# Eight expert tiles listed early and interleaved with the attention tail

## The chip, the cores and the metric
One core of a Trainium2 chip runs the whole program in one launch. The metric is the device time of the launch in microseconds (us); the time before is the median of three runs.

## What is computed
Two layers over x of shape (32, 128, 256), that is 4096 tokens of width 256. Each layer adds a gated cross attention (16 heads of 16) and then a gated mixture of experts (8 experts, two per token) to x:

```python
x = x + tanh(g_xattn) * attention(layernorm(x), ctx)
h = layernorm(x)
x = x + tanh(g_ffn) * experts(h)     # top 2 of 8, by a router on h
```
In layer 0 an expert is a relu network of width 1024 with biases and the gates are a softmax of the two best logits. In layer 1 the attention is causal and masked, an expert is silu(gate) * up of width 512, and the gates come from masked softmaxes (two exponentials over all eight logits).

## The kernel before
There are five instruction lists, written by hand, one for each engine (TensorE, VectorE, ScalarE, GpSimd, SyncE); each engine runs its own in order and waits on semaphores. Each layer has two stages.

**Attention** runs over steps s from FIRST = -8 to LAST = 148 (`pe_attention`, L492, and its like for the other engines). A unit is four heads of one batch, 128 units in all; a step handles unit s, and the pieces of the neighbouring units that are due. `grp(s, k)` and `bat(s, k)` say whether the piece of a group (4 batches, 8 groups) or of a batch is due k steps behind its start. The last units end at step 127; behind it come sums, the last outputs, and the routing of the last groups.

**Routing** of a group (`Part`, L114) starts at step `e0`: the reciprocal root of the variance (started on VectorE, 12 small instructions on GpSimd, L903 to L909, for groups 0 to 6), the normed rows XR (L1208), two transposes, the logits (L566), maximum and index (L970, L975), SEL (L988), gates (L993 to L1032), ranks by two matmuls (L572), the running counts CR and the row numbers PI (L1039 to L1060). GpSimd then scatters the rows to the expert's region in DRAM, one DMA_INDIRECT per 128 rows (L1403), eight for a group. The last group is routed in two halves, and its root is made on VectorE. `dve_lists` (L1233) makes, when all groups are counted, where the rows of each tile start: tiles 0 to 7 are the first tile of each expert, tiles 8 to 38 come from the list, whose expert and start SyncE reads into registers (L1437, L1455). `pad` (L785) writes 256 rows behind the end of each expert's rows.

**Experts** runs over NT = 39 tiles of 256 rows. The work of tile i on TensorE (L627): the transposes of tile i + 1's rows (`pe_turn_x`, L578), the up projection of tile i in four pieces q, the down projection of tile i - 1. Every product is three matmuls, high x high, high x low, low x high (L420 to L422). ScalarE rounds the weights to their high parts (`act_w`, L791), and makes relu or silu and the hidden high parts (L812, L826). VectorE makes the low parts of the rows, of the hidden values and of weight quarters 1 and 2; GpSimd makes the low parts of quarters 0 and 3 (`low_w`, L1273) and scatters the outputs (`pool_y`, L1406). Tile i + 1's up projection needs quarter 0's low part; the down projection needs quarters 2 and 3. SyncE's iteration i (L1552) asks for the rows of tile i + 2 first and then for biases and the weight quarters, each once its buffer is free. Two row buffers and two weight generations are in turn.

Ahead of the experts stage TensorE waits until all banks are free (`banks_out`, L396) and runs WARM2 = 48 matmuls on nothing (L630). SyncE asks for tile 0's rows when the last group's scatters have landed; the pads of experts 1 to 3 are issued by ScalarE, the others by SyncE.

Of the kernel before, what the change touches and what calls it, by code (L numbers as in the profile page):

```python
# [15 lines left out]
T = B * S  # L16
E = 8
# [5 lines left out]
NT = (2 * T - E) // TS + E  # L23
ROW = D + 2
# [10 lines left out]
WARM, WARM1, WARM2 = 8, 28, 48  # L35
# [8 lines left out]
C_TOK = C_TILE + NT - E  # L44
# [4 lines left out]
def constants():  # L49
# [9 lines left out]
    c[:, C_TILE:C_TILE + NT - E] = np.arange(NT - E)  # L59
# [51 lines left out]
class Part:  # L111


    def __init__(self, g, lo, hi):  # L114
# [3 lines left out]
        late = g >= NG - 2  # L118
# [3 lines left out]
            self.e1 + k for k in ((1, 1, 1, 1, 1, 2, 2, 3, 3, 3) if late else (1, 2, 2, 3, 3, 4, 3, 4, 5, 6)))  # L122
# [19 lines left out]
def bat(s, k):  # L142
    b, m = divmod(s - k, 4)
    return b if m == 0 and 0 <= b < B else None


def program(nc, A):
    ctx = ExitStack()
    with ctx:  # L149
# [37 lines left out]
        su = sb("su", [128, NT - E])  # L187
# [25 lines left out]
        tge = sb("tge", [128, NT - E, E])  # L213
        tv = sb("tv", [128, 4, NT - E])
        tvi = sb("tvi", [128, 2, NT - E], I32)
# [7 lines left out]
        HS = [v.rearrange("p (z f n) -> p z f n", z=2, f=8) for v in (PTR[:, 0:4096], WR[:, :, :, :, :].rearrange("p w z t n -> p (w z t n)"))]  # L223
# [3 lines left out]
        b2s = XRf[:, 6 * D:8 * D].rearrange("p (r d) -> p r d", r=2)  # L227
# [3 lines left out]
        XN = U2[:, 1024:2048].rearrange("p (g d) -> p g d", g=G)  # L231
        XR2 = U2[:, 2048:2048 + 2 * G * ROW].rearrange("p (k g d) -> p k g d", k=2, g=G)
# [11 lines left out]
        SB_, PTB, OB, BK, BO_, HBK, YB, XB = PS[0:3], PS[3:5], PS[5], PS[6], PS[7], PS[0:4], PS[4:6], PS[6:8]  # L244
# [4 lines left out]
        def xr(g):  # L249
            return XR if g < NG - 1 else XR2  # L250

# [48 lines left out]
        p_rs2 = mark("p_rs2", [k for k in prts if k[1] < NG - 1])  # L300
# [8 lines left out]
        v_pd, v_tl = mark("v_pd", LL), mark("v_tl", LL)  # L309
# [27 lines left out]
        def uses_bk(L):  # L337
            out = []
            for s in range(FIRST, LAST):
# [18 lines left out]
            return out  # L358
# [36 lines left out]

        def banks_out(w, L):  # L396

            w.wait_ge(*a_p[L, NU - 1])
            w.wait_ge(*a_pt[L, NU - 1])
            w.wait_ge(*v_on[L, B - 1])  # L400
            w.wait_ge(*a_v[L, NG - 1, 1])
            w.wait_ge(*v_rk[(L,) + PARTS[-1].key])
            w.wait_ge(*v_lg[(L,) + PARTS[-1].key])
            if L == 0:
                w.wait_ge(*v_xup[0, B - 1])
# [85 lines left out]

        def pe_attention(e, w, L):  # L492
            pe_first(e, w, L)
            for s in range(FIRST, LAST):
                if 0 <= s < NU:
                    i, bank = s, pt_place["p", s]
                    w.wait_ge(*a_p[L, i])
                    turn_free(w, L, "p", i)
                    for h in range(4):
                        ins = e.transpose(bank[:, h * 128:(h + 1) * 128], PB[:, i % 3, h], ident)  # L500
                    ins.then_inc(*m_t(L, i))
                if 0 <= s + 4 < NU:
                    i = s + 4
                    b, m, z = i // 4, (i // 2) % 2, i % 2
                    g, j, bank = b // G, b % G, SB_[i % 3]
                    w.wait_ge(*v_q[L, g, 1])
                    if i < 2:
                        w.wait_ge(*a_v[L, 0, i])
                    w.wait_ge(*d_k[key_queue(L, b)][L, b, 7])
                    if i >= 3:  # L510
                        w.wait_ge(*a_p[L, i - 3])
# [8 lines left out]
                if (b := bat(s, 6)) is not None:  # L520
# [3 lines left out]
                    for n in range(4):  # L524
                        ins = e.transpose(bank[:, n * 128:(n + 1) * 128], OS[:, n * 128:(n + 1) * 128], ident)
# [1143 lines left out]
```

## Time and profile before
| | |
|---|---|
| median of three runs | 1687.52 us (1686.19 to 1691.3) |
| profiled execution, first to last instruction | 1689.9 us |
| TensorE busy | 1575.0 us, 93% |
| VectorE, ScalarE, GpSimd busy | 71%, 73%, 49% |
| mean granted TensorE clock | 0.966 |
| DMA | 256.56 MB, mean 152 GB/s |

Times are us from the span's start. A granted clock of 1 is 2.4 GHz, 0.5 is 1.2 GHz. The chip's profile page gives only this span for the profiled execution; the three runs are separate ones. Layer 0's attention fills 0 to about 356, its experts 410 to about 880, layer 1's attention then runs to about 1256 and its experts from 1318 to the end.

### The profile page before, as it was taken

Reading aid. Unit: us, or ns where it says so; the run is one execution under the profiler, and the core shown is the slowest. Engines: PE = TensorE matmul, PEld = TensorE weight load, DVE = VectorE, ACT = ScalarE, POOL = GpSimd, SP = SyncE. Lnnn points to the kernel's source line nnn. Section 1 sums busy time; section 2 is a strip of 40 time slices with the busy share of each in tenths; the row PEclk is TensorE's granted clock in tenths of the full one; section 3 lists DMA queues with packets and bytes.
Section 4 is the critical chain, followed back from the end, with each engine's and each line's share of the span. In section 5 each row is a group of like instructions: output and inputs, shape, how many; then the busy total and the mean of one; then the engine's idle time right before and its main releaser. Section 6 shows DMA issues by size and latency. Waiting matters only on the chain. (4 is left out here: it accounts for less than half of the span.)

```text
span 1689.9 us, 37219 instructions
## 1 busy us (share of the span) xinstructions
PE 1575.0 (93%) x12832; PEld 1424.2 (84%) x12832; DVE 1194.5 (71%) x2829; ACT 1232.1 (73%) x2859; POOL 826.4 (49%) x887
## 2 busy tenths in 40 slices
PE   7999999976999999999988999999984999999996
PEld 5788888865999999999986777777773899999996
DVE  5677777755777777777766788888857566766664
ACT  5888888853888888888863877777771577777774
POOL 3224444343556565656552113333323477777776
PEclk9999999987999999999998999999995999999999
DMA  3222222135877777778742223333232788788883
GB/s 110 54 50 75 75 76 76 51 95 148 261 235 235 224 230 228 232 226 236 225 141 78 72 82 104 107 104 104 62 90 77 200 225 242 222 230 231 226 233 99
DMA packets 208988, 256.56 MB, mean 152 GB/s; under 512 B 29555, under 2 KB 156788, under 8 KB 208800
## 3 DMA queue, kind: packets, MB, share of 16 engines
q1 hardware_dynamic: 185408, 217.95, 44.2%
q0 software_dynamic: 21120, 34.39, 7.9%
q10 hardware_dynamic: 2272, 1.85, 0.4%
q8 instruction: 102, 1.67, 0.4%
q14 instruction: 86, 0.70, 0.1%
HBM read 194.54 MB, written 45.74 MB: 142 GB/s over the span
## 5 line engine op out<-in xcount | busy, mean ns | idle before, releaser
L1276 POOL TENSOR_TENSOR KXR<-U,KXR 128x1024 fp32r<-128x1024 f32 (+1 forms) x156 | 355.2, 2277 | 276.9 <-ACT KXR L795 276.9
L420 PE MATMUL ps<-QR,KXR 128*128 128x256 f32 x1248 | 360.4, 289 | 0.8 <-DVE QR L1280 0.7
L422 PE MATMUL ps<-QR,KXR 128*128 128x256 f32 x1248 | 354.2, 284 | 0.0
L421 PE MATMUL ps<-QR,KXR 128*128 128x256 f32 x1248 | 354.0, 284 | 0.0
L795 ACT ACTIVATE KXR<-U 128x1024 fp32r<-128x1024 f32 (+1 forms) x312 | 287.4, 947 | 73.2 <-PE ps L422 49.4
L743 ACT ACTIVATE U<-ps,mx 128x128 f32<-128x128 f32 x1024 | 299.0, 405 | 20.3 <-DVE mx L1153 20.3
L420 PEld LDWEIGHTS ps<-QR,KXR 128*128 128x128 f32 x1248 | 240.6, 193 | 1.4 <-DVE QR L1280 1.3
L421 PEld LDWEIGHTS ps<-QR,KXR 128*128 128x128 f32 x1248 | 240.4, 193 | 0.0
L422 PEld LDWEIGHTS ps<-QR,KXR 128*128 128x128 f32 x1248 | 240.0, 192 | 0.0
L1153 DVE TENSOR_REDUCE mx<-ps 128x4 f32<-128x512 f32 x256 | 174.3, 684 | 69.3 <-PE ps L422 37.1
L1276 DVE TENSOR_TENSOR KXR<-U,KXR 128x1024 fp32r<-128x1024 f32 (+1 forms) x156 | 175.0, 1160 | 25.6 <-ACT KXR L795 25.5
L1403 POOL DMA_INDIRECT xs_scr<-XR,PI x112 | 109.8, 980 | 133.6 <-DVE PI L1060 104.6
L500 PE MATMUL ps<-cst,U 128*128 128x128 f32 x1024 | 163.5, 283 | 10.0 <-DVE U L1163 9.5
L750 ACT ACTIVATE U<-ps 128x512 f32<-128x512 f32 x256 | 166.5, 650 | 7.4 <-PE ps L500 7.4
L500 PEld LDWEIGHTS ps<-cst,U 128*128 128x128 f32 x1024 | 117.3, 143 | 48.1 <-issue 23.6
L821 ACT ACTIVATE U<-ps,b1s 128x256 f32<-128x256 f32 x312 | 130.4, 473 | 29.9 <-PE ps L422 29.9
L1307 DVE TENSOR_TENSOR PTR<-U,PTR 128x512 fp32r<-128x512 f32 x80 | 101.0, 1298 | 60.6 <-ACT PTR L832 60.6
L420 PE MATMUL ps<-KXR,PTR 128*128 128x256 f32 x480 | 136.1, 284 | 3.6 <-ACT U L810 1.5
L1307 DVE TENSOR_TENSOR WR<-U,WR 128x512 fp32r<-128x512 f32 x76 | 97.9, 1326 | 56.6 <-ACT WR L832 56.6
L421 PE MATMUL ps<-KXR,PTR 128*128 128x256 f32 x480 | 135.8, 283 | 0.0
L422 PE MATMUL ps<-KXR,PTR 128*128 128x256 f32 x480 | 135.8, 283 | 0.0
L1419 POOL DMA_INDIRECT out<-U,xi x78 | 121.1, 1552 | 20.0 <-issue 19.7
(206 smaller groups left out, 4043.3 us busy)
## 6 DMA issues: line engine op xcount, KB each, us to landing
U<-in_wpack SPq DMA_DIRECT2D x234, 512.0 KB, 4.4
U<-in_wpack SPq DMA_DIRECT2D x78, 256.0 KB, 4.2
KXR<-U SPq DMA_DIRECT2D x504, 32.0 KB
U<-xs_scr SPq DMA_DIRECT2D x39, 258.0 KB, 4.5
U<-xs_scr SPq DMA_DIRECT2D x39, 257.0 KB, 4.7
U<-in_ctx_t SPq DMA_DIRECT2D x16, 512.0 KB, 5.7
U<-ys_scr SPq DMA_DIRECT2D x32, 256.0 KB, 3.4
XR<-in_L_ffn_b SPq DMA_DIRECT2D x39, 128.0 KB, 3.9
```

Source lines behind the costliest of these rows:

```text
L420: e.matmul(o, wh, xh, start=first, stop=False)
L421: e.matmul(o, wh, xl, start=False, stop=False)
L422: return e.matmul(o, wl, xh, start=False, stop=done)
L500: ins = e.transpose(bank[:, h * 128:(h + 1) * 128], PB[:, i % 3, h], ident)
L743: ins = e.activation(PB[:, i % 3, h], SB_[i % 3][:, h * 128:(h + 1) * 128], ACT.Exp, bias=mx[:, i % 4, h:h + 1], scale=-1.0)
L750: e.activation(PT[:, i % 3].rearrange("p h k -> p (h k)"), pt_place["p", i][:, :], ACT.Copy).then_inc(*a_pt(L, i))
L795: e.activation(w_cols(L, WH, n), w_raw(L, n), ACT.Copy).then_inc(*a_w[n](L, i))
L821: ins = e.activation(HB[:, r, f], HBK[q][:, z * 256:z * 256 + 256], ACT.Relu, bias=b1s[:, r, f:f + 1])
L1153: e.tensor_reduce(mx[:, i % 4], SB_[i % 3][:, :].rearrange("p (h k) -> p h k", h=4), AX.X, ALU.min).then_inc(*v_mx(L, i))
L1276: e.tensor_tensor(w_cols(L, WL, n), w_raw(L, n), hi, ALU.subtract).then_inc(*l_w[n](L, i))
L1307: ins = e.tensor_tensor(low[:, 2 * q:2 * q + 2], HB[:, i % 2, 2 * q:2 * q + 2], high[:, 2 * q:2 * q + 2], ALU.subtract)
L1419: ins = e.indirect_dma_start(ys_d[1], at, yo[:, r, a, :], None, bounds_check=T - 1, oob_is_err=False, compute_op=ALU.add)
```

## The change
- KE = 8 tiles are listed from the counts of the first GE = 5 groups (20 batches), in steps 101 to 104 (`dve_lists_early`). Only full tiles are taken, so none needs padding; an assertion says that eight always exist. The rest, tiles 8 to 38, is listed from the final counts less those tiles, in steps 147 to 149. NT stays 39.
- Attention's own loop ends at START = 128. Steps 128 to 149 are run inside the expert loop, four to a tile, so inside tiles 0 to 5: step 128 + 4 i + k is piece k of tile i (`late`). On each engine they stand between the pieces of a tile.
- The rows of tiles 0 and 1 are requested in step 117, transposed in steps 124 and 126; two weight quarters of tile 0 are rounded there too, and their low parts made (steps 125 and 126, on GpSimd and VectorE).
- The bank wait and the 48 matmuls go; the tile transposes take turns in the two banks that attention's projections and the routing use.
- The last group is routed whole, its reciprocal root on GpSimd like the others.
- All eight pads are issued by SyncE in iteration 6 of the experts stage, and the rows of tile 8 are requested at its end. The expert and start of every tile come from registers.
- The output biases and part of the hidden buffers move to other memory.

```diff
+GE, KE = 5, 8
-PARTS = [Part(g, 0, G) for g in range(NG - 1)] + [Part(NG - 1, 0, G // 2), Part(NG - 1, G // 2, G)]
+PARTS = [Part(g, 0, G) for g in range(NG)]
-FIRST, LAST = -8, 148
+FIRST, START, LAST = -8, 128, 150
+LIST0, TX, LIST1 = 101, (124, 126), 147
...
+def late(i, k):
+
+    s = START + 4 * i + k
+    return s if s < LAST else None
...
         def pe_experts(e, w, L):
-            banks_out(w, L)
-            for n in range(WARM2):
-                e.matmul(SB_[2][:, :], QR[:, 0, 0, 0, 0:128], QR[:, 1, 0, 0, :], start=True, stop=True)
-            for i in range(2):
-                pe_turn_x(e, w, L, i)
-            for i in range(NT):
-                if i and i + 1 < NT:
+            for q in range(4):
+                pe_up(e, w, L, 0, q)
+                pe_late(e, w, L, 0, q)
+            for i in range(1, NT):
+                if i + 1 < NT:
                     pe_turn_x(e, w, L, i + 1)
-                pe_up(e, w, L, i)
-                if i:
-                    pe_down(e, w, L, i - 1)
+                for q in range(4):
+                    pe_up(e, w, L, i, q)
+                    if q % 2:
+                        pe_late(e, w, L, i, q // 2)
+                for half in range(2):
+                    pe_down(e, w, L, i - 1, half)
+                    pe_late(e, w, L, i, 2 + half)
             pe_down_last(e, w, L)
...
+            for s in range(FIRST, START):
+                act_step(e, w, L, s)
+                for i in range(2):
+                    if s == TX[i]:
+                        act_w(e, w, L, 0, i)
+                        act_turn_x(e, w, L, i)
...
+            for s in range(FIRST, START):
+                dve_step(e, w, L, s)
+                for i in range(2):
+                    if s == TX[i] + 1:
+                        dve_turn_x(e, w, L, i)
+                if s == TX[1]:
+                    low_w(e, w, L, 0, 1)
...
         def dve_experts(e, w, L):
-            dve_lists(e, w, L)
-            low_w(e, w, L, 0, 1)
...
+                    if i == 0:
+                        dve_late(e, w, L, 0, q)
+                    elif q == 1:
+                        dve_late(e, w, L, i, 0)
                 if L == 1:
                     dve_hidden(e, w, 1, i, 3)
+                if i:
+                    dve_late(e, w, L, i, 1)
                 if i + 1 < NT:
                     low_w(e, w, L, i + 1, 1)
+                if i:
+                    dve_late(e, w, L, i, 2)
                 low_w(e, w, L, i, 2)
+                if i:
+                    dve_late(e, w, L, i, 3)
...
         def pool_experts(e, w, L):
-            low_w(e, w, L, 0, 0)
             for i in range(NT):
                 if i:
                     low_w(e, w, L, i - 1, 3)
+                pool_late(e, w, L, i, 0)
                 if i >= 2:
                     pool_y(e, w, L, i - 2)
+                pool_late(e, w, L, i, 1)
                 if i + 1 < NT:
                     low_w(e, w, L, i + 1, 0)
+                for k in (2, 3):
+                    pool_late(e, w, L, i, k)
...
         def sp_experts(e, w, L):
-            pad(e, w, L, 0)
...
-            for x in range(4, E):
-                pad(e, w, L, x)
             for i in range(NT):
+                if L == 1 and i == 1:
+                    sp_store_x(e, w, NG - 1)
+                if i == KE - 2:
+                    for x in range(E):
+                        pad(e, w, L, x)
-                if L == 0 and i == 2:
+                if L == 0 and i == KE + 2:
                     sp_ahead(e)
...
-                if i + 2 < NT:
+                if i + 2 < NT and i + 2 != KE:
                     sp_fetch_x(e, w, L, i + 2)
...
                 if i + 1 < NT:
                     sp_fetch(e, w, L, i + 1, 2, sp_expert(e, w, L, i + 1))
+                if i + 2 == KE:
+                    sp_fetch_x(e, w, L, KE)
```
ScalarE's list has the late steps at the same places as VectorE's (`act_late`). GpSimd's step code and the step code of the other engines is the old code moved into functions (`pe_step`, `act_step`, `dve_step`, `pool_step`).

## Rows read from the trace of the kernel before

**Rows 1.** 40 us stretches: busy us (x instructions) per engine, PEclk, DMA share, GB/s
```profile
core 0: us, PE busy (x) PEld busy (x) DVE busy (x) ACT busy (x) POOL busy (x), PEclk, DMA share, GB/s
360.00:400.00 40.00, 24.37 (x140) 19.86 (x139) 25.10 (x141) 7.61 (x18) 16.61 (x21) 0.62 0.17 58
...
600.00:640.00 40.00, 40.00 (x337) 40.00 (x337) 30.24 (x35) 31.63 (x55) 22.43 (x13) 1.00 0.77 224
...
1280.00:1320.00 40.00, 24.21 (x102) 19.79 (x103) 23.43 (x125) 7.57 (x15) 17.37 (x18) 0.66 0.39 128
...
1440.00:1480.00 40.00, 40.00 (x337) 40.00 (x337) 27.21 (x57) 30.07 (x65) 30.59 (x19) 1.00 0.83 236
```

**Rows 2.** TensorE's timeline, layer 0: start, us, engine, line, operation, [idle before <-releaser]
```profile
359.18 0.66 PE L558 MATMUL ps<-cst,XR 128*128 128x128 f32 x4 [2.97 <-DVE XR L1208]
...
394.54 13.22 PE L630 MATMUL ps<-QR 128*128 128x512 f32 x48 [0.28 <-DVE RK L965]
...
494.05 0.60 PE L585 MATMUL ps<-cst,U 128*128 128x128 f32 x4
...
506.00 0.60 PE L585 MATMUL ps<-cst,U 128*128 128x128 f32 x4
```

**Rows 3.** TensorE's timeline, layer 1
```profile
1267.48 0.64 PE L488 MATMUL ps<-U,VA 128*32 128x128 f32 x16
...
1383.50 0.60 PE L585 MATMUL ps<-cst,U 128*128 128x128 f32 x4
...
1392.57 0.60 PE L585 MATMUL ps<-cst,U 128*128 128x128 f32 x4
```

**Rows 4.** ScalarE's timeline, layer 0's tail
```profile
362.60 1.05 ACT L775 ACTIVATE XR<-XR 128x1024 f32<-128x1024 f32 x1
```

**Rows 5.** VectorE's timeline: routing in both tails, hidden pieces of two tiles
```profile
370.90 0.23 DVE L965 COPY RK<-ps 128x64 f32<-128x64 f32 x1
...
373.01 0.17 DVE L1060 CAST PI<-PF 128x8 int32<-128x8 f32 x1
...
584.01 4.44 DVE L1307 TENSOR_TENSOR PTR<-U,PTR 128x512 fp32r<-128x512 f32 x3 [1.08 <-ACT PTR L832]
...
1267.59 0.19 DVE L959 COPY LG<-ps 128x32 f32<-128x32 f32 x1 [3.48 <-PE ps L566]
...
1269.44 0.19 DVE L988 TENSOR_TENSOR SEL<-MM 128x32 f32<-128x32 f32 x1
...
1271.61 0.18 DVE L1009 TENSOR_SCALAR rt<-rt 128x32 f32<-128x32 f32 x1
...
1480.18 0.42 DVE L1309 TENSOR_TENSOR WR<-ps,WR 128x256 fp32r<-128x256 f32 x1 [1.42 <-ACT WR L834]
```

**Rows 6.** GpSimd's timeline: reciprocal root, scatters, output scatters, low weights
```profile
351.08 0.22 POOL L903 TENSOR_TENSOR rs<-rsi 128x4 f32<-128x4 f32 x1
...
354.19 0.20 POOL L909 TENSOR_TENSOR rs<-rs 128x4 f32<-128x4 f32 x1
...
374.84 0.97 POOL L1403 DMA_INDIRECT xs_scr<-XR,PI  x1 [0.30 <-issue]
...
581.67 1.26 POOL L1417 DMA_INDIRECT ys_scr<-U,xi  x1 [0.15 <-issue]
...
584.23 2.45 POOL L1276 TENSOR_TENSOR KXR<-U,KXR 128x1024 fp32r<-128x1024 f32 x1
...
1477.40 1.56 POOL L1419 DMA_INDIRECT out<-U,xi  x1 [0.16 <-issue]
...
1480.27 2.98 POOL L1276 TENSOR_TENSOR KXR<-U,KXR 128x1024 fp32r<-128x1024 f32 x1
```

**Rows 7.** SyncE's timeline: four pads in a row, the rows of a tile
```profile
409.10 4.76 SPq L788 DMA_DIRECT2D xs_scr<-cst  x4
...
580.12 0.38 SPq L1468 DMA_DIRECT2D U<-xs_scr  x1
```

**Rows 8.** DMA issues of the page: tile rows in layer 0, KB each, us to landing
```profile
U<-xs_scr SPq DMA_DIRECT2D x39, 257.0 KB, 4.7
```

**Rows 9.** ScalarE's timeline, start of layer 1's experts
```profile
1318.85 1.28 ACT L824 ACT_TABLE_LOAD   x1
```

More of the change, by code:

```diff
@@ L117, in __init__ @@
         self.e0 = 16 * g + 4 * hi + 9
-        late = g >= NG - 2
+        fast = g >= NG - 2
         self.lt = (self.e0 + 4, self.e0 + 5)
@@ L338, in uses_bk, with uses_step @@
             out = []
-            for s in range(FIRST, LAST):
+            for s in range(FIRST, START):
+                uses_step(L, s, out)
+                for i in range(2):
+                    if s == TX[i]:
+                        out.append((("tx", i), v_x[L, i]))
+            for k in range(4):
+                uses_step(L, late(0, k), out)
+            for i in range(1, NT):
+                if i + 1 < NT:
+                    out.append((("tx", i + 1), v_x[L, i + 1]))
+                for k in range(4):
+                    if (s := late(i, k)) is not None:
+                        uses_step(L, s, out)
+            return out
+        def uses_step(L, s, out):
                 for name, at, empty in (("xt", X0, v_xt), ("q", Q0, v_q), ("k", K0, v_k), ("v", V0, a_v)):
@@ new lines, in pe_up, with pe_rows, pe_down @@
+            ins.then_inc(*m_h(L, i, q))
+        def pe_rows(e, w, L, i, f, a):
+            nf, c = NFs[L], (2 * F0, 4 * F1)[L] + f * D
+            w.wait_ge(*v_h[L, i, f if L else f // 2])
+            w.wait_ge(*l_w[2 + 2 * f // nf][L, i])
+            high, low = (hs(i, z, f, f + 1)[:, 0, a * 128:a * 128 + 128] for z in range(2))
+            return three(e, YB[a][:, 0:D], (high, low), (WH[:, c:c + D], WL[:, c:c + D]), f == 0, f == nf - 1)
+        def pe_down(e, w, L, i, half):
+            nf = NFs[L]
@@ L1315, in dve_gated, with dve_late @@
             e.tensor_tensor(up, HB[:, i % 2, q], up, ALU.mult).then_inc(*v_hm(i, q))
+        def dve_late(e, w, L, i, k):
+            if (s := late(i, k)) is not None:
+                dve_step(e, w, L, s)
         def dve_experts(e, w, L):
-            dve_lists(e, w, L)
-            low_w(e, w, L, 0, 1)
-            for i in range(2):
-                dve_turn_x(e, w, L, i)
             for i in range(NT):
@@ L1406, in pool_y, with pool_attention, pool_late @@
+        def pool_attention(e, w, L):
+            pool_first(e, w, L)
+            for s in range(FIRST, START):
+                pool_step(e, w, L, s)
+                if s == TX[0] + 1:
+                    low_w(e, w, L, 0, 0)
+        def pool_late(e, w, L, i, k):
+            if (s := late(i, k)) is not None:
+                pool_step(e, w, L, s)
         def pool_y(e, w, L, i):
```

848 lines of the change are left out of this document (456 added, 392 removed).

## The prediction
> **What bounds the kernel now.** I read the stretches of 40 us first. In the expert stages TensorE is busy for the whole stretch (40.00 of 40, 337 matmuls, so 0.119 us each); at 360 to 400 and at 1280 to 1320 it is busy for 24 us of 40 and its granted clock is 0.62 and 0.66 [rows 1]. These two stretches are the tails between attention and experts. Then I read TensorE's own timeline there. Layer 0: its attention work thins out at 356; its next matmul, at 359.18, follows 2.97 us of idleness; at 394.54 come 48 matmuls that only keep the clock up (13.2 us); tiles 7 and 8 start at 494.05 and 506.00 [rows 2]. Layer 1: the sum of the last unit is at 1267.48, tiles 7 and 8 start at 1383.50 and 1392.57 [rows 3]. A tile takes 11.95 us in layer 0 (100 matmuls) and 9.07 in layer 1 (76). The eight tiles ahead of tile 8 are the stretch that the change rearranges; behind it nothing changes. So I compute when tile 8 starts in each layer and compare.
>
> **The gross gain.** What is left of the tail (steps 128 to 149) is a few us of TensorE work: 4.1 us in layer 0 and 3.3 in layer 1 behind tile 0 (transposes, logits, ranks, the last output projection), and in tile 0 some 3 and 1.5. In layer 1 the first up projection could start at about 1268.0, where the last sum was. In layer 0 it is later than that sum. ScalarE ends the copy at 363.65 [rows 4]; behind it stands the new rounding of weights (1.05 us, the same 128x1024 form of copy); VectorE now waits for it inside attention to form the low part (1.2), then does its step 127 (1.3), on whose X update the bank of the second tile transpose waits (0.6); then the last transposes and the logits (2.3). That gives 370.0. Without any further wait tile 8 would start at 370.0 + 8.9 + 7 x 11.95 + 4.1 = 466.7 in layer 0, 39.3 us earlier than now, and at 1268.0 + 7.3 + 7 x 9.07 + 3.3 = 1342.1 in layer 1, 50.5 us earlier. Sum 89.8 us. The 48 matmuls per layer and the half groups' second square root are in this sum and are not counted again.
>
> **What it gives back.** Each engine runs its list in order, and the late steps stand between the pieces of a tile.
>
> *Tiles 0 and 1.* The ranks of group 6 are made in step 129. VectorE: 2.0 us from the logits' copy to SEL, 2.3 us from the rank copy to the row numbers, in layer 1 another 2.2 us for the gates [rows 5]. ScalarE waits in its step 128 for those gates and holds back the hidden columns. I come to the row numbers 15.1 us behind tile 0's start in layer 0 and 16.0 in layer 1. Then GpSimd issues four scatters (0.97 + 0.30 each, so 5.1 us), forms the low weights of tile 0's last quarter (2.4; half of it in layer 1), issues four more and forms tile 2's first quarter (2.45 to 2.98) [rows 6]. Tile 2 starts at +30.1 and +30.2, against 21.2 and 16.8 without waits: 8.9 and 13.4 lost.
>
> *Tile 2.* Step 137 has VectorE start group 7's reciprocal root and GpSimd do 12 instructions, 3.3 us [rows 6]. VectorE gets there when its four hidden pieces and the statistics are done, 11.9 us into the tile in layer 0 (the pieces q1 to q3 end at 588.4, and that tile starts at 506.00 + 6 x 11.95 = 577.7, so 10.7 us into it) [rows 2, 5] and 9.4 in layer 1. The low weights of tile 3's first quarter are queued on GpSimd behind it: 11.9 + 3.3 + 2.45 = 17.7, wanted at 12.3, and 15.3 against 9.4. Lost 5.4 and 5.9.
>
> *Tiles 4 and 5.* Step 144 is the routing of group 7. It stands behind the second hidden piece, so TensorE, done with its up projection at 6.2, waits for SEL until about 9.4 (8.2 in layer 1, where the first piece is ready at 1480.6, in a tile that starts at 1392.57 + 9 x 9.07 = 1474.2, so 6.4 us into it) [rows 3, 5]. The row numbers come at +17.8 and +18.8, since the hidden pieces, the gates and one low part stand between. Behind them on GpSimd: four scatters 5.1, low weights 2.4 (1.3), two scatters 2.5, two output scatters 2.55 (3.4), two scatters 2.5, low weights 2.45 (2.7) [rows 6]; 17.5 us in each. Tile 6 can start at +35.3 and +36.3, against 24.8 and 19.0: 10.5 and 17.3 lost. GpSimd is busy for 30.59 of 40 us in layer 1 already [rows 1].
>
> *Tile 8's rows.* Now the rows of a tile are requested at the start of the iteration two tiles ahead, 580.1 in the tile of 577.7, so 2.4 us into it and 9.5 before TensorE turns them [rows 7]. For tile 8 the change requests them at the end of iteration 6, behind all eight pads, and TensorE turns them at the start of iteration 7. On SyncE: start 3.0, eight pads at 1.19 (four took 4.76) 9.5, bias loads 2.3, four weight loads and the rows 5.7: issued at +20.5 in layer 0, landing 4.7 us later [rows 7, 8], at +25.2, where TensorE is ready at +11.6. In layer 1 there are no bias loads: I take +22.5 against +8.7. Lost 13.6 and 13.8. This is the surest term, since every price in it is a row.
>
> *Clock.* After an idle gap the granted clock is half: the tails show 0.62 and 0.66 [rows 1]. Where TensorE is not the one waited for, a slow matmul costs nothing; behind the long wait at tile 8 I take 1.5 us per layer. Bounds: 0, and 27 for the rival below.
>
> *Small terms.* In layer 1 the gates' Exp now stands between Silus: two changes of table and back, 1.28 us each [rows 9], within ScalarE's waits above, nothing more. The Trainium skill (ScalarE: Activation LUTs, What ACT_TABLE_LOAD costs) adds a drain and says about 2.66 us per switch; by it the sum would be some 3 us longer at two switches on the chain, and no row here shows the drain. The early lists (22 small VectorE instructions in steps 101 to 104, about 0.2 us each in chain, so 4.4 us a layer) lie beside attention, where TensorE leads in layer 0 and VectorE is close in layer 1; I take 2 us in all, bounds 0 and 9. SyncE reads the expert from a register in tiles 0 to 7, which it did not; it has the time, 1.15 us an issue, except in the term above. The burst of layer 1's loads, moved from tile 2 to tile 10, costs its 1.0 us outside the stretch. Scatters and pads, 4 MB a layer, join a DMA load of 0.77 [rows 1]; I take nothing, bounds 0 and 6, as the pads' own issue is already the slowest part.
>
> A low-weight instruction on GpSimd takes 2.45 us in layer 0 and 2.98 in layer 1, where VectorE's work overlaps it otherwise [rows 6]. The Trainium skill (SBUF — State Buffer, Who interferes with whom) says that a VectorE instruction with two SBUF inputs and a GpSimd one exclude each other for a whole instruction; by it VectorE's routing, with two small inputs in most instructions, could hold GpSimd back at each of its pieces, 0.5 us by the difference of the two rows, 4 to 6 us over both layers. I have it in the range only.
>
> **The sum.** Given back, layer 0: 8.9 + 5.4 + 10.5 + 13.6 + 1.5 = 39.9; layer 1: 13.4 + 5.9 + 17.3 + 13.8 + 1.5 = 51.9. With 2.0 and 1.0 it is 94.8 against 89.8, so 5.0 us slower. The profiled execution spans 1689.9 us; 1694.9. The median of the runs, 1687.5, lies 2.4 below that execution: 1692.5. A measurement of this kernel tells about 0.3%, 5 us, from no change, so this is within it, at the slow edge.
>
> **Rivals.**
> *Faster.* The routing waits (50.1 us over tiles 0 to 6 without the root) overlap more than I chain them, for instance because ScalarE and VectorE are ahead when a late step comes. For it: all three have idle time in layer 0 (VectorE 9.8, ScalarE 8.4, GpSimd 17.6 of 40 us, rows 1). Against: the lists are in order, and the waits come from order, not from load. The clock, the root and tile 8's rows stay. If half of the 50.1 go: 1667; if all: 1642. Chance 0.36.
> *Slower, by the clock.* TensorE is stopped at four places per layer, and each stop puts it at half clock as in the two tails. Tiles 0 to 7 hold 96 and 73 us of its work; if a third of it runs at 1.2 GHz, 56 us more, of which I take half to fall into waits: +27, 1719. It decides when the granted clock of these tiles is below 0.85. For it: 0.62 in a stretch with 24 us of work [rows 1]. Against: the stops are short beside a tile's 11.9 us of matmuls. The Trainium skill (TensorE: Matmul & The Clock Gate, HAM oscillation) tells of this pattern, where repeated gaps put the array back to the low clock each time. Chance 0.24.
> *Forecast.* The waits eat the gain, 1680 to 1706. Chance 0.40, the likeliest single case.
> That fewer tiles are listed is excluded: eight full tiles always exist in five groups, and the number of tiles stays 39.
>
> **How the numbers follow.** Forecast 1692. The range takes in half of the routing waits and most of the all-go case below (1645), and the clock rival with its DMA bound above (1722). Over 5 us faster: 0.38, the first rival and the low edge of my case; within: 0.20, from my case; slower: 0.42, the rest of it and the second rival.
>
> **What would show it.** Right: no idle stretch as in the two tails, but TensorE waits at the starts of tiles 2 and 3 and 6 for GpSimd's low weights, and some 13 us in each layer for DMA of the tile's rows at one transpose; DMA_INDIRECT of the routing back to back on GpSimd in front of these; the first up projection near 370 and 1268. Wrong: that 13 us wait absent, or the waits on GpSimd together under 25 us, or a granted clock below 0.85 over the eight tiles.

## The result, and the profile after

The changed kernel takes **1724.42 us** (median of 4 runs, 1721.84 to 1727.66) against 1688.54 for the kernel before, a ratio of 1.0212 with a 95% interval of 1.0191 to 1.0233. The forecast was 1692 in a range of 1645 to 1722, so the kernel is 36 us slower than before where 4 to 5 were forecast, and lies 2 us outside the range. The profiled execution spans 1725.9 us; by the sum it should have spanned 1694.9. So 31.0 us are to be found in the trace.

The stretches of 40 us, columns as in [rows 1]:
```profile
core 0: us, PE busy (x) PEld busy (x) DVE busy (x) ACT busy (x) POOL busy (x), PEclk, DMA share, GB/s
...
360.00:400.00 40.00, 28.81 (x206) 27.10 (x207) 22.53 (x61) 20.96 (x40) 14.23 (x12) 0.83 0.28 80
400.00:440.00 40.00, 29.53 (x217) 28.91 (x217) 26.76 (x39) 24.05 (x43) 24.32 (x27) 0.87 0.63 198
440.00:480.00 40.00, 32.83 (x263) 32.39 (x261) 26.05 (x76) 23.51 (x39) 19.64 (x14) 0.96 0.51 145
480.00:520.00 40.00, 23.70 (x163) 23.53 (x164) 11.82 (x15) 16.18 (x31) 17.21 (x11) 0.74 0.69 199
...
1360.00:1400.00 40.00, 25.78 (x172) 24.80 (x172) 24.97 (x97) 17.49 (x39) 24.25 (x18) 0.74 0.52 137
1400.00:1440.00 40.00, 25.79 (x194) 25.59 (x194) 15.17 (x31) 17.78 (x39) 14.94 (x10) 0.79 0.66 172
```
One stretch with 24 us of work has become four with 24 to 33, and no engine is full in any of them. That speaks for a chain and not a load, and the experiments below test it. Which waits make it is in the table of TensorE's waits, layer 0 from 360 to 525 and layer 1 from 1283 to 1430 (us in total, times, longest):
```profile
PE ps L444 <- issue: 12.7, 2, 7.0
PE ps L614 <- DMA U<-xs_scr: 12.1, 1, 12.1
PE ps L594 <- DVE SEL L1042: 6.1, 2, 4.4
PE ps L614 <- DVE X L1004: 4.4, 1, 4.4
PE ps L580 <- DVE OT L1000: 4.2, 1, 4.2
PE ps L444 <- DVE OT L1000: 3.8, 2, 2.1
PE ps L580 <- DVE U L1257: 2.7, 1, 2.7
...
PE ps L444 <- issue: 17.2, 3, 7.9
PE ps L614 <- DMA U<-xs_scr: 16.2, 2, 14.2
```
The waits are 47 us in layer 0 and 52 in layer 1. L614 is the transpose of a tile's rows, L594 the rank matmul, L580 the transposes of the normalized group, L444 the first matmul of an up or down projection. Where L444 shows "issue", its inferred releaser is missing; GpSimd's timeline (below) shows its low weights ending there. In time order (layer 0, then layer 1):
```profile
362.05 1.09 PE L580 MATMUL ps<-cst,XR 128*128 128x128 f32 x4 [4.24 <-DVE OT L1000]
...
370.98 0.63 PE L614 MATMUL ps<-cst,U 128*128 128x128 f32 x4 [4.37 <-DVE X L1004]
...
372.11 3.42 PE L588 MATMUL ps<-rw,U 128*128 128x8 f32 x16
375.39 0.56 PE L444 MATMUL ps<-QR,KXR 128*128 128x256 f32 x1
...
407.72 0.60 PE L614 MATMUL ps<-cst,U 128*128 128x128 f32 x4
...
425.91 0.55 PE L444 MATMUL ps<-QR,KXR 128*128 128x256 f32 x1 [5.68 <-issue]
436.21 0.90 PE L580 MATMUL ps<-cst,U 128*128 128x128 f32 x4 [2.67 <-DVE U L1257]
...
484.21 0.55 PE L444 MATMUL ps<-QR,KXR 128*128 128x256 f32 x1 [7.00 <-issue]
509.53 1.12 PE L614 MATMUL ps<-cst,U 128*128 128x128 f32 x4 [12.09 <-DMA U<-xs_scr]
...
1392.49 0.55 PE L444 MATMUL ps<-QR,KXR 128*128 128x256 f32 x1 [7.86 <-issue]
1416.94 1.12 PE L614 MATMUL ps<-cst,U 128*128 128x128 f32 x4 [14.21 <-DMA U<-xs_scr]
```
The transposes at 509.53 and 1416.94, done at the start of iteration 7, are tile 8's; tile 8's own iteration starts with those at 523.97 and 1428.72. Before, that was at 506.00 and 1392.57 [rows 2, 3], so layer 0 hands on 18.0 us and both layers together 36.2. SyncE's timeline shows why tile 8's rows are late: eight pads, the bias loads, four weights, and only then the rows (the second of the two at L1606 is tile 9's):
```profile
487.14 9.55 SPq L833 DMA_DIRECT2D xs_scr<-cst  x8
...
499.75 3.20 SPq L1582 DMA_DIRECT2D U<-in_wpack  x4
504.11 1.59 SPq L1606 DMA_DIRECT2D U<-xs_scr  x2
```
GpSimd's timeline in tile 2 of layer 0, the root and the low weights behind it:
```profile
418.06 1.09 POOL L957 TENSOR_TENSOR rs<-rsi 128x4 f32<-128x4 f32 x1 [3.80 <-DVE rsi L939]
419.24 1.06 POOL L959 TENSOR_TENSOR rs<-rs 128x4 f32<-128x4 f32 x1
420.38 0.19 POOL L961 TENSOR_SCALAR rs<-rs 128x4 f32<-128x4 f32 x1
...
423.44 4.75 POOL L1384 TENSOR_TENSOR KXR<-U,KXR 128x1024 fp32r<-128x1024 f32 x2
```
GpSimd stands 3.80 us for VectorE's start of the root, spends 5.0 on it (3.3 in [rows 6]), and the low weights of tile 3 end at about 425.8, where TensorE resumes.

### The profile page after: what moved, and what is told of

Same layout as the page of the kernel before. It is cut to its first block and busy times, and to the rows that moved or that the text cites. A ratio compares the mean times of both kernels' runs of the same rounds, so it can differ in the third digit from the quotient of the medians.

```text
span 1725.9 us, 37428 instructions
## 1 busy us (share of the span) xinstructions
PE 1562.6 (91%) x12728; PEld 1419.0 (82%) x12728; DVE 1187.1 (69%) x2778; ACT 1233.7 (71%) x2854; POOL 832.5 (48%) x907
## 5 line engine op out<-in xcount | busy, mean ns | idle before, releaser
L1384 POOL TENSOR_TENSOR KXR<-U,KXR 128x1024 fp32r<-128x1024 f32 (+1 forms) x156 | 350.0, 2245 | 308.0 <-ACT KXR L840 301.3
L444 PE MATMUL ps<-QR,KXR 128*128 128x256 f32 x1248 | 368.9, 296 | 32.3 <-issue 29.9
L445 PE MATMUL ps<-QR,KXR 128*128 128x256 f32 x1248 | 360.9, 289 | 0.0
L446 PE MATMUL ps<-QR,KXR 128*128 128x256 f32 x1248 | 360.8, 289 | 0.0
L444 PEld LDWEIGHTS ps<-QR,KXR 128*128 128x128 f32 x1248 | 248.0, 199 | 34.6 <-issue 31.5
L445 PEld LDWEIGHTS ps<-QR,KXR 128*128 128x128 f32 x1248 | 248.0, 199 | 0.0
L446 PEld LDWEIGHTS ps<-QR,KXR 128*128 128x128 f32 x1248 | 247.3, 198 | 0.0
L522 PE MATMUL ps<-cst,U 128*128 128x128 f32 x1024 | 164.0, 283 | 10.5 <-DVE U L1215 10.0
L1417 DVE TENSOR_TENSOR PTR<-U,PTR 128x512 fp32r<-128x512 f32 x80 | 97.1, 1244 | 79.8 <-ACT PTR L881 79.6
L444 PE MATMUL ps<-KXR,PTR 128*128 128x256 f32 x480 | 137.8, 287 | 7.8 <-POOL KXR L1384 5.4
L1426 DVE TENSOR_TENSOR ps<-U,ps 128x256 f32<-128x256 f32 x156 | 70.3, 450 | 88.3 <-ACT U L873 87.8
```

The lines of the kernel that those rows point to most:

```text
L444: e.matmul(o, wh, xh, start=first, stop=False)
L445: e.matmul(o, wh, xl, start=False, stop=False)
L446: return e.matmul(o, wl, xh, start=False, stop=done)
L1384: e.tensor_tensor(w_cols(L, WL, n), w_raw(L, n), hi, ALU.subtract).then_inc(*l_w[n](L, i))
```

## The experiments

Theory A: the loss is waits that come from the order of each engine's list. Theory B: the clock behind the stops is the main loss. Theory C: the early lists cost much. Times are medians; unless said otherwise a difference is against the changed kernel's 1724.4. The experiments ran later than the changed kernel, each beside the kernel before, and that one then had medians of 1690.4 to 1692.3, not 1688.5. So a difference of the two ratios comes out 0.2 to 6 us more in favour of an edit than a difference of medians. It is given where it changes the reading.

**e1, pads early.** In `sp_experts` the pads stand behind `sp_fetch(i, 3)` of iteration 5 and no longer at the head of iteration 6; tile 8's rows are requested at the usual place.
```diff
+                if i == KE - 3:
+                    for x in range(E):
+                        pad(e, w, L, x)
-                if i == KE - 2:
-                    for x in range(E):
-                        pad(e, w, L, x)
-                if i + 2 == KE:
-                    sp_fetch_x(e, w, L, KE)
```


> Edit: SyncE issues the eight pads in iteration 5, ahead of tile 7's weights, and requests tile 8's rows at the start of iteration 6 like every other tile's. Theory A (waits made by the order of the queues): the waits of 12.1 and 14.2 us at tile 8's transposes go, since the rows need only the last scatters (near 483 in layer 0) and are wanted at 497; about 26 us less, 1724 becomes 1698, between 1692 and 1704. Rival R1 (another wait takes its place: the pads now stand ahead of tile 7's weights on SyncE): half of it comes back as a wait at tile 7's up projection, 1706 to 1714. Theory B (the clock is the main loss): the wait alone is worth under 20 us and the granted clock of 480 to 520 stays near 0.74.

Measured: 1697.9 (1692.5 to 1702.1), ratio to the kernel before 1.0054 [1.0035, 1.0073]; 26.5 us less. SyncE issues the pads where it would wait anyway:
```profile
472.70 9.87 SPq L833 DMA_DIRECT2D xs_scr<-cst  x8
483.34 2.16 SPq L1582 DMA_DIRECT2D U<-in_wpack  x3
491.72 0.38 SPq L1606 DMA_DIRECT2D U<-xs_scr  x1
```
The wait at tile 8 falls from 12.09 to 0.46 us in layer 0 and goes in layer 1; no other took its place. Tile 8's iteration starts 12.0 us behind its transposes (496.63 to 508.63) and not 14.4, so the longest stop cost 2.4 us more than its length; in layer 1 it is 9.1 and not 11.8. The granted clock of 480 to 520 is 0.92 where it was 0.74, against B's expectation.

**e2, the root of group 7 on VectorE**, as the kernel before had it for its last groups.
```diff
+                    if p.g == NG - 1 and s == p.e0 + 2:
+                        w.wait_ge(*v_rs2[k])
+                        dve_rsqrt(e, w, 1, p.js)
```


> Edit: group 7's reciprocal root is made by VectorE (nine small instructions in chain, in step 139) and not by GpSimd in step 137. Theory A: low weights of tile 3's first quarter are no longer queued behind a root of 5.0 us; the waits at tile 3's up projection (5.68 and 6.46 us) shrink to under 2, VectorE pays about 2 us elsewhere: 6 to 10 us less in both layers together, 1714 to 1718. Rival R2 (nothing gained, since VectorE's root of about 2 us stands ahead of its own low weights and hidden pieces, and the next stop takes it): 1722 to 1726.

Measured: 1715.2, 9.2 us less. By the ratios it is 10.5. The 5.68 and 6.46 us at tile 3's up projection are gone; the wait for the normalized rows grows from 2.67 to 4.05 in layer 0 and from 1.48 to 4.15 in layer 1. VectorE's timeline of this run shows what delays these rows:
```profile
416.30 3.65 DVE L1420 TENSOR_TENSOR PTR<-U,PTR 128x512 fp32r<-128x512 f32 x1 [1.06 <-ACT PTR L881]
...
424.34 2.37 DVE L946 TENSOR_TENSOR rs<-rsi 128x4 f32<-128x4 f32 x1
...
427.14 0.16 DVE L946 TENSOR_TENSOR rs<-rs 128x4 f32<-128x4 f32 x1
```
and GpSimd's:
```profile
416.92 2.46 POOL L1387 TENSOR_TENSOR KXR<-U,KXR 128x1024 fp32r<-128x1024 f32 x1
423.31 3.39 POOL L1387 TENSOR_TENSOR KXR<-U,KXR 128x1024 fp32r<-128x1024 f32 x1 [3.92 <-ACT KXR L840]
```
A hidden piece that takes 0.69 us elsewhere in this stretch takes 3.65, and the root's first instruction on 128x4 takes 2.37. The first ends at 419.95, 0.6 us behind the end of a low-weight instruction of GpSimd (419.38), the second at 426.71 with the end of the next one (426.70).

**e3, low weights ahead of the late pieces on GpSimd.**
```diff
+                if i + 1 < NT:
+                    low_w(e, w, L, i + 1, 0)
+                if i:
+                    for k in (2, 3):
+                        pool_late(e, w, L, i - 1, k)
+                for k in (0, 1):
+                    pool_late(e, w, L, i, k)
```


> Edit: GpSimd forms the low weights of tile i+1's first quarter ahead of every late piece of iteration i, and the late pieces 2 and 3 move into the next iteration behind that too; nothing else moves. Theory A: the waits of TensorE for GpSimd's low weights at the up projections of tiles 2, 3 and 6 go (5.68 + 7.00 in layer 0, 2.86 + 6.46 + 7.86 in layer 1, 29.9 us in all), a third of it returns as waits for the later row numbers or for the up projection's own cover: 18 to 24 us less, 1700 to 1706; tile 8's wait stays 12 to 14 us. Rival R3 (the scatters of group 7, now a tile later, become what tile 8's rows wait for): the wait at tile 8 grows by what is saved, under 10 us less, 1714 or more. Theory B: under 10 us less, as the clock stays low.

Measured: 1711.9, 12.5 us less, between A and R3. The wait at tile 6 goes from 7.00 to 3.11 us (now inside its down projection) and from 7.86 to 0.86. But in layer 0 the normalized rows wait longer for the root (6.05, not 2.67), and the waits for tile 8's rows grow to 13.16 and 17.30 us, as SyncE's pads are not moved here. Counted from the first up projection, TensorE is ready for these rows 5.5 us earlier in layer 0 and 12.4 in layer 1 than in the changed kernel, and they land 4.5 and 9.3 us earlier. So the wait for them swallows 4.2 of 17.9 us, not all: much of SyncE's list waits for the other engines too and moves with them.

**e4 and e14, the clock.** In e4 TensorE does 12 unused matmuls in the wait at tile 8:
```diff
+                if i == KE - 1:
+                    bank_free(w, L, "tx", i + 1)
+                    for n in range(12):
+                        e.matmul(place[L, "tx", i + 1][:, :], ident, cst[:, 0:512], start=True, stop=True)
```


> Edit: in the wait at tile 8's transposes TensorE does 12 matmuls of 512 columns whose result is not used (about 10 us at full clock), in both layers; they end ahead of the rows' landing. It measures what the clock costs behind the longest stop. Theory A: 1 to 2.5 us per layer, 1719 to 1722. Theory B (the clock is the main loss): 5 us or more per layer, 1714 or less, and the granted clock of 480 to 520 rises to 0.9 or more. Rival: no gain, since the matmuls end late and push the transposes: 1724 or more.

e14 adds 5 ahead of tile 3's up projection and 7 ahead of tile 6's:
```diff
+            if q == 0 and i in (3, 6):
+                w.wait_ge(*(v_h[1, i - 1, q] if L else a_h[0, i - 1, q]))
+                for n in range(5 if i == 3 else 7):
+                    e.matmul(HBK[q][:, :], ident, cst[:, 0:512], start=True, stop=True)
```

> Edit: the changed kernel as it is, with matmuls whose result is not used in three of its waits per layer: 5 ahead of tile 3's up projection, 7 ahead of tile 6's, 12 ahead of tile 8's transposes (0.85 us each at full clock); each set ends inside its wait. Theory A (a stop costs about 1 us more of half clock behind it, as the one stop filled in e4 gave 0.8 us per layer): 2 to 5 us less than the changed kernel's 1724.4, 1719 to 1722. Theory B (the clock is a main loss beside the waits): 10 us or more less, 1714 or below.

Measured: e4 1722.8 (1719.0 to 1723.2), 1.7 us less, 2.5 by the ratios; e14 1724.1 (1721.4 to 1725.9), 0.3 less, 3.5 by the ratios (1.0191 [1.0178, 1.0205] against 1.0212 [1.0191, 1.0233]). Neither can be told from nothing, nor from the 2 to 5 us of A; the 10 us of B are excluded. The stretches of e14:
```profile
400.00:440.00 40.00, 33.31 (x229) 30.19 (x228) 24.06 (x37) 24.82 (x45) 26.91 (x28) 0.91 0.65 206
...
1320.00:1360.00 40.00, 33.00 (x236) 29.70 (x234) 22.32 (x58) 20.21 (x40) 25.42 (x27) 0.96 0.59 159
1360.00:1400.00 40.00, 34.17 (x200) 28.62 (x201) 24.92 (x85) 19.27 (x42) 22.08 (x16) 0.87 0.55 150
1400.00:1440.00 40.00, 35.11 (x234) 30.22 (x233) 15.55 (x36) 18.30 (x41) 18.71 (x12) 0.96 0.72 186
```
In layer 1 it is 0.96, 0.87, 0.96 from 1320 on, where the changed kernel has 0.83, 0.74, 0.79. What became of that is seen at tile 3 of layer 0: its up projection takes 6.0 us at full clock (1.00 from 428.6 to 434.6), 7.6 in the changed kernel (0.75); then the wait for the normalized rows is 3.08 us and not 2.67, and behind it the clock is 0.74 and not 0.83, and the passes take 10.8 us and not 9.9. To tile 4 it is 19.9 us and not 20.2. So most of what was won went at the next wait. Tile 8's rows land 26.0 us behind tile 6's up projection in e14 (486.81 to 512.81), 25.3 before.

The fill was not complete, though: e14's matmuls end 4.00 and 4.89 us ahead of those rows, and in layer 0 the passes behind them are as slow as before (14.5 us to the next tile, granted clock 0.81 in both). In e4, where 2.81 and 2.00 us are left, the same stretch takes 13.5 us at 0.87 in layer 0 and 9.1 at 1.00 in layer 1, against 14.4 and 11.8. There TensorE is what the others wait for, and the half clock costs 0.9 and 2.6 us. B, as the main loss, falls; that the clock is worth nothing is not shown. The Trainium skill (TensorE: Matmul & The Clock Gate, HAM oscillation) describes the half clock behind repeated gaps; the rows agree that it is there (a set of 128x256 passes 0.21 us apart where others are 0.12).

**e6, the early lists twice.**
```diff
+                if s == LIST0 - 4 + n:
+                    dve_lists_early(e, w, L, n, True)
```


> Edit: the 22 small VectorE instructions of the early lists stand twice, the second set four steps earlier on the counts of four groups, its results unused. It doubles the cost of the early lists beside attention. Theory A: 2 us in layer 0 and 2 in layer 1 are what one set costs, so 1726 to 1730. Theory C (the early lists are a main loss): 10 us or more on top, 1734 or more. Rival: hidden wholly, 1724.

Measured: 1732.1, 7.6 us more, between A and C; by the ratios (1.0238 [1.0213, 1.0263]) it is 4.4, which is A. So a set costs some 2 to 4 us per layer, where the prediction took 1. The traces put 3.7 us of it in layer 0, where group 6's transposes come at 365.78 and not 362.05. In steps 101 to 104 VectorE is late for the next group's first transposes and projections; TensorE's waits from 285 to 345 in the changed kernel:
```profile
PE ps L459 <- DVE PTR L970: 1.5, 1, 1.5
PE ps L444 <- DVE PTR L970: 0.8, 1, 0.8
...
```
Before, the longest wait there was 0.4 us.

**e7, tile 0's low weights behind step 127**, that is behind VectorE's loop over the attention steps.
```diff
-                if s == TX[1]:
-                    low_w(e, w, L, 0, 1)
+            low_w(e, w, L, 0, 1)
```


> Edit: VectorE forms the low weights of tile 0's second quarter behind step 127 and the split of tile 1, and not ahead of step 127's X update. Theory A (the bank of tile 1's transposes waits for that update, 4.37 us in layer 0): the first up projection of layer 0 comes 1.2 to 3 us earlier, layer 1 (no output projection there) 0 to 1: 1720 to 1723. Rival: the low weights are then late for the third part of tile 0's up projection, no gain: 1724 or more.

Measured: 1715.3, 9.1 us less (12.3 by the ratios), more than twice the most that was expected. The wait of 4.37 us goes, and with it a second loss, layer 0:
```profile
366.71 0.66 PE L614 MATMUL ps<-cst,U 128*128 128x128 f32 x4
...
367.64 1.85 PE L588 MATMUL ps<-rw,U 128*128 128x8 f32 x16
369.34 0.36 PE L444 MATMUL ps<-QR,KXR 128*128 128x256 f32 x1
```
The 16 logit matmuls take 1.85 us, not the 3.42 at half clock behind the stop: here nothing hides them. The first up projection is 6.0 us earlier (369.34, not 375.39). The remaining 3.1 us, or 6.3 by the ratios, I could not put to one place; they stay open.

**e8, group 7's ranks one step later.**
```diff
+        if g == NG - 1:
+            self.rk, self.rank, self.rows, self.scatter = self.e1 + 3, self.e1 + 4, self.e1 + 4, self.e1 + 4
-LIST0, TX, LIST1 = 101, (124, 126), 147
+LIST0, TX, LIST1 = 101, (124, 126), 148
```


> Edit: group 7's ranks, row numbers, scatters and the late lists come one step later (ranks in step 146 in place of 145); TensorE's rank matmul then stands behind the first half of tile 3's down projection. Theory A (TensorE stands for SEL because it reaches the rank too early, 4.37 us in layer 0, 2.09 in layer 1): these two waits go, at most 1 us of them is left, and the later scatters give 0 to 3 us back per layer at tile 6's up projection or tile 8's rows: 1718 to 1724. Rival R8 (what counts is when the row numbers come, not where TensorE waits): the wait at tile 6's up projection or at tile 8's rows grows by as much or more, 1724 to 1730.

Measured: 1720.3, 4.1 us less. The wait for SEL falls from 4.37 to 1.54 us in layer 0, the one at tile 6 rises from 7.00 to 8.15; in layer 1 it is 2.09 to 0.71 and 7.86 to 9.12. A net gain smaller than the wait removed, as A says.

**e5, e1 to e3 together.**

> Edit: the three edits of e1, e2 and e3 together. Theory A (each is a wait of its own in an ordered chain, so they add up, and the longer wait that e3 showed for the X halves of step 140 behind GpSimd's root, 6.05 us in place of 2.67, goes with the root on VectorE): 1724 less 26.5, 9.2 and 12.5, and 2 to 6 more, gives 1670 to 1676, faster than both kernels. Rival R5 (they overlap: with the pads early and the scatters of group 7 a tile later, the rows of tile 8 wait for the scatters): 1683 to 1690.

Measured: 1695.4 over 12 runs, 1.0023 [1.0008, 1.0037]; the three gains sum to 48.2 and 29.0 came. R5 was nearest in time, though the time lies 5 us above its range. Waits at tile 8's transposes are back, 4.73 and 7.68 us, and SyncE's waits from 470 to 493 name what is late:
```profile
SPq L109 <- DMA xs_scr<-cst: 6.3, 4, 2.1
SPq L109 <- DMA xs_scr<-U,PI: 2.3, 1, 2.3
```
So it is the pads' landing first (issued from 468.9 to 478.4) and then, by 2.3 us more, the scatters'. So even issued early the pads can be what the rows wait for, by their transfer. TensorE comes to tile 8's transposes 7 us earlier than in e1 (489.2 against 496.2), and the rows are requested at the same time in both, 491.0 and 491.7.

**e9, e1 with e2 and e7.**

> Edit: the edits of e1 (pads early), e2 (root on VectorE) and e7 (low weights of tile 0 behind step 127) together, GpSimd's order left as the change has it. Theory A, corrected by e5 (the last scatters must not come later, since with the pads early they are what tile 8's rows wait for): the three gains add up, 1724 less 26.5, 9.2 and 9.1 gives 1680, 1676 to 1684, faster than both kernels by 10 and 44 us. Rival: a wait for the scatters at tile 8 here too, as in e5: 1688 or more.

Measured: 1683.2 (1678.8 to 1685.2), 0.9945 [0.9924, 0.9966]: faster than both kernels, and 41.2 us less than the changed one where the three gains sum to 44.8 (45.1 and 49.5 by the ratios). So three waits that come from the order of the lists, with what hangs on them, are worth more than the whole loss of 36 us.

**Four edits on top of e9.** e10 adds e8's edit.

> Edit: e9 with group 7's ranks, scatters and late lists one step later (e8's edit). In e8 it took 2.8 us off the SEL wait of layer 0 and brought 4 us. Theory A: here the scatters are on the path to tile 8's rows, so it gives nothing or costs: e9 to e9 plus 4. Rival: they have slack, and it brings 3 to 4 us again.

Measured: 1686.8, 0.9954 [0.9939, 0.9970]: nothing gained, as A says; the wait at tile 6 is 8.16 us (5.64 in e9), and the same edit that gave 4.1 us alone gives none here.

e11 turns tiles 0 and 1 one step later:
```diff
-LIST0, TX, LIST1 = 101, (124, 126), 147
+LIST0, TX, LIST1 = 101, (125, 127), 147
...
+            dve_turn_x(e, w, L, 1)
             low_w(e, w, L, 0, 1)
```

> Edit: e9 with the transposes of tiles 0 and 1 one step later each (steps 125 and 127 in place of 124 and 126), so that of the two shared banks none of them takes the bank of an output projection that VectorE has yet to read. Theory A (the start of tile 0 in layer 0 is a chain of bank waits: 4.2 us ahead of group 6's transposes): first up projection of layer 0 comes 2 to 4 us earlier, layer 1 unchanged: e9 less 2 to 5. Rival (the wait is VectorE's work itself, whatever bank is asked for): within 1 us of e9.

Measured: 1685.6, 0.9967 [0.9949, 0.9986], no gain. The first up projection is 8.2 us behind group 6's transposes (362.19 to 370.38), 7.1 in e9 (360.59 to 367.71). The bank wait is replaced by one for VectorE's normalized rows, and there is a new one of 2.51 us at the next use of the bank pair:
```profile
362.19 0.66 PE L580 MATMUL ps<-cst,XR 128*128 128x128 f32 x4 [2.49 <-DVE XR L1260]
```
The rival holds, and the bank is not what sets this start. VectorE's rows of the changed kernel name what does:
```profile
359.06 0.74 DVE L1257 TENSOR_SCALAR XR<-X,mv,rs 128x256 f32<-128x256 f32 x2 [4.77 <-issue]
```
VectorE stands idle 4.77 us before the first normalized half of group 6. Its list waits there for the landing of group 5's last scatter, which is still read from the same buffer. GpSimd issues that scatter at 351.91, and the half starts 7.15 us later; in e11 it is 353.14 and 7.02, in e9 350.61 and 6.99, in the kernel before 350.10 and 7.05. The profile names no releaser, so this rests on the list and on the constant distance.

e12 moves group 6's last scatters alone behind the low weights (e3's edit for iterations 0 and 1):
```diff
+                if i == 1:
+                    low_w(e, w, L, 2, 0)
+                    for k in (2, 3):
+                        pool_late(e, w, L, 0, k)
```

> Edit: e9 with group 6's last two pairs of scatters behind the low weights of tiles 0 and 2 on GpSimd (e3's edit for group 6 alone; group 7's stay). Theory A (the waits at tile 2 and 3 of layer 1, 2.9 us left of them with the root gone, come from those scatters, and nothing waits for group 6's scatters before tile 8): 2 to 4 us less than e9. Rival (in layer 0 the ready XR2 and X update pieces move later and take it back, as in e3): e9 or more.

Measured: 1683.7, 0.9959 [0.9941, 0.9977], no gain: layer 1's wait of 3.18 us at tile 2's up projection (e9) is gone, and one of 4.92 stands at tile 3's, where e9 has none. The wait moved.

e13 cuts the four pieces of the early lists into eight (steps 101 to 108), the same instructions in the same order:
```diff
-            for n in range(4):
+            for n in range(8):
                 if s == LIST0 + n:
                     dve_lists_early(e, w, L, n)
```

> Edit: e9 with the 22 instructions of the early lists in eight steps (101 to 108) and not in four. e6 showed that a second set costs 7.6 us in both layers. Theory A (a step is late by what VectorE adds to it, and several small additions are hidden where few larger ones are not): half of one set's cost comes back, 2 to 5 us less than e9. Rival (VectorE's work is the pace of these steps, spread or not): within 1.5 us of e9.

Measured: **1676.9** (1674.6 to 1681.7), 0.9921 [0.9906, 0.9935]; 6.3 us less than e9 by the medians, 4.1 by the two ratios, whose intervals overlap. It has the lowest time of the study. In layer 0 the stretch's longest wait is now 0.80 us, 1.5 in e9:
```profile
306.70 0.66 PE L459 MATMUL ps<-cst,U 128*128 128x128 f32 x4 [0.80 <-DVE PTR L970]
```
But the traces do not show layer 0 earlier by it: group 5's scatters start at 341.23, in e9 at 340.99. So the time and the waits fit a gain from the spreading, as A says, and where it arises is open.

e15 has the root on VectorE in step 138:
```diff
-                    if p.g == NG - 1 and s == p.e0 + 2:
+                if p.g == NG - 1 and s == p.e0 + 1:
```

> Edit: e9 with VectorE's root of group 7 in step 138 and not in 139. In e9 TensorE waits 4.04 and 4.14 us for the X halves at step 141's transposes. Theory A: they come up to 2 us earlier, since in step 138 VectorE is ahead: 2 to 4 us less than e9. Rival (the root then stands ahead of tile 3's low weights, which are wanted first): within 1 us of e9, or more than e9.

Measured: 1682.1, 0.9946 [0.9928, 0.9964]: as e9. The wait for the normalized rows stays (3.89 and 4.14 us), so what delays them is not the root's place within tile 2.

## Why the prediction was wrong

Its **mechanism was right**: the idle tail becomes ordered waits that eat the whole gain. What it gave as signs came, the 12 to 14 us at tile 8's transposes and waits for GpSimd's low weights of 34 us in all; one of its signs of being wrong came too, the granted clock over the eight tiles, 0.86 in layer 0 (375.39 to 523.97) but 0.80 in layer 1 (1291.73 to 1428.72), bound 0.85. Its **sizes** were short by 31.0 us. The terms that failed are tile 3, which had none and was 9.3 us over, the start of tile 0 in layer 0 (5.4), and, in both, a clock that was priced behind tile 8's rows alone. The rival that came out nearest in time, 1719 by the clock, was so by luck for the most part: it wanted 27 us from the clock, and filling stops gave 0 to 4 us (e14, e4).

Step by step, layer 0 first; each figure is the trace's start minus the forecast's.

- *Tile 8's rows* (13.6 and 13.8 forecast). Landing 25.3 and 24.5 us behind tile 6's up projection, forecast 25.2 and 22.5. Right to 0.1 and 2.0 us, and shown by e1 to be worth the full wait.
- *Start of tile 0*: 370.0 forecast, 375.39 in layer 0: **5.4 short**. The step that failed is "ScalarE ends the copy at 363.65". The copy ends at 367.6. Of these 4.0 us, 1.9 are the later landing of group 5's scatters (VectorE's normalized halves at 359.06, 357.15 before), 1.0 the bank of the pair that tile 0's transposes now share, and 1.1 transposes at half clock behind the stop. How much of the 1.9 the early lists cost is not settled: in traces of kernels with the same lists, group 5's scatters start at 340.9 to 343.5, 342.29 here, 340.46 before. The chain behind the copy was as written, but its logits ran at half clock, 3.42 us in place of 1.85. Layer 1 was right: 7.9 us behind the transposes of group 6, 8.0 forecast.
- *Tiles 0 and 1* (8.9 and 13.4): 32.3 and 30.8 us to tile 2, forecast 30.1 and 30.2. Short by 2.2 and 0.6.
- *Root in tile 2* (5.4 and 5.9): 0.9 and 2.6 short. The root took 5.0 us, not 3.3.
- *Tile 3, which had no term*: from its up projection to tile 4 (446.12) it took 20.2 us in layer 0, where the terms give 14.4 (a tile and the late steps' work), and 14.7 in layer 1 where they give 11.2; **9.3 us short**, the largest miss. The normalized halves of group 7 stand behind the root on VectorE's list (2.67 and 1.48 us). The rest, some 5 us, is half clock behind the stops, with TensorE the one waited for: the up projection takes 7.6 and 7.7 us, where e14 has 6.0 at full clock in both layers, and the passes behind the second stop of layer 0 ran at 0.83. I had priced the root for the low weights queued behind it, and not for the second work that waits for it, nor the clock behind its stop.
- *Tiles 4 and 5* (10.5 and 17.3): tile 6 at +38.1 and +37.3, forecast 35.3 and 36.3. Short by 2.8 and 1.0, where VectorE and GpSimd work at once.
- *Behind tile 8's rows*: 14.4 and 11.8 us to the next tile, forecast 14.3 and 10.6. Short by 1.3, mostly clock.
- *Small terms*: lists, burst and the way from one layer to the next 5.9 us, of which 3.0 were forecast. In it are the burst of loads, 2.03 us of wait at one tile's transposes (1.0 taken), and layer 1's early lists, 2 to 4 us by e6's times but 1.2 by its trace. It can't be closed: the way from tile 8 of layer 0 to group 6's transposes of layer 1 is 759.9 us here and 754.0 before, and 755.1 to 767.5 in the traces of the experiments that leave it as it is.
- *Table loads* (nothing taken). In layer 1 they lie in ScalarE's waits, except that TensorE waits 3.80 us for the copy of the last sums, which ScalarE holds back for the gates, as the prediction had it in the term of tiles 0 and 1. The load takes 1.28 us and the next ACTIVATE follows at once:
```profile
1298.57 0.21 ACT L819 ACTIVATE rt<-rt 128x32 f32<-128x32 f32 x1
1298.80 1.28 ACT L873 ACT_TABLE_LOAD   x1
1300.09 0.38 ACT L873 ACTIVATE U<-ps 128x256 f32<-128x256 f32 x1
```
The Trainium skill (ScalarE: Activation LUTs, What ACT_TABLE_LOAD costs) gives about 2.66 us per switch with a drain; the instruction ahead of this load ends at 1298.78, so here a switch is 1.3 us in all, and the measurement decides.

The misses are 17.3 us in layer 0, 10.9 in layer 1 and 2.9 between, which makes the 31.0, as it must, since they are cut from one trace: which part would come again in another execution is not shown. Nearly all terms erred to one side. The walk priced each piece as if it ran alone on its engine, and gave no place to a wait that it had not found; the range's slow end had too little room for that.

## What to carry to other kernels

When work is threaded between the pieces of other work, walk every engine's list for who waits behind each moved piece, and look twice at a result with two waiters (the root: low weights and normalized rows). Of each wait, ask how far it moves with the work ahead of it and how far it is set by a queue such as the pads': the second part swallows savings made ahead of it (4.2 of 17.9 us in e3), so it goes first (e1). Edits were worth 26.5, 9.2 and 9.1 us alone and 41.2 together, while others (e10, e12) only moved a wait. A granted clock is read as a price where TensorE is what the others wait for (0.9 and 2.6 us behind tile 8's rows, e4); elsewhere the next wait takes most of it (e14). And a comparison of runs taken at different times goes by the ratios to the kernel that ran beside both: the medians alone would read 4 us as nothing in e14 and 4 us as nearly 8 in e6.

## What the runs showed of the hardware

- **Two engines that hold each other up.** VectorE's small root instruction took 2.37 us beside GpSimd's low weights and 0.16 alone (e2); GpSimd's 1.09 and 1.06 beside VectorE's low weights, 0.20 alone (418.06 and 419.24 above). A VectorE hidden piece took 3.65 us against 0.69. The prediction had this in the range only, and for GpSimd's side only, at 4 to 6 us. That one of the two stands for the other's whole instruction is what the Trainium skill says (SBUF — State Buffer, Who interferes with whom); the rows agree, in both directions, and by up to 3.0 us a piece.
- **Half clock costs what is exposed.** 16 logit matmuls took 3.42 us behind a stop of 4.37 us and 1.85 without it, on the path. Tile 3's up projection took 7.6 us at a granted clock of 0.75 and 6.0 at 1.00, but with another wait close behind it tile 4 came only 0.3 us sooner (e14).
- **Pads are DMA work, too.** Issued in 9.9 us in e1, a pad landed 5.6 to 9.6 us behind its issue, and SyncE stood for them until 491.7, 9 us behind the last issue; in e5 they, more than the scatters, held tile 8's rows.
- **A scatter's landing holds the next write into its source.** From the issue of a group's last scatter to the first write into its buffer it is 7.0 to 7.2 us in the four traces named at e11, and TensorE stood 2.5 to 4.2 us at the transposes behind that write. That it is the landing follows from the list's wait; the profile names no releaser.
